# The last two head groups of a gated cross-attention block, run by halves of the batch, with four expert tiles between them

## The chip, the cores and the metric

One core of a Trainium2 chip runs the whole kernel. The metric is the device time of one execution in microseconds (us). The engines are TensorE (PE, matrix products), VectorE (DVE), ScalarE (ACT), GpSimd (POOL) and SyncE (SP), which issues the DMAs. Each executes its own list of instructions in order, and they meet at semaphores.

## The reference

Eight batches of 128 tokens with 512 features. Everything is fp32.

```
x = x + tanh(g_xattn) * attention(layernorm(x), ctx, ctx, pos, mask)
x = x + tanh(g_ffn)  * moe(layernorm(x))

attention: q = h @ Wq (32 heads of 128); k, v = ctx @ Wk, ctx @ Wv (8 heads); rotary on q and k
           softmax(q k' / sqrt(128), masked) v, then @ Wo
moe:       gate = softmax([h, mean|text| / mean|vision|] @ gate_w + gate_b), the two best of 3 experts
           expert e: act_e(h @ w1[e] + b1[e]) @ w2[e] + b2[e],  act = tanh, gelu, silu
           the experts of a batch are those that its token 0 picks
```

## The kernel before

**Products.** Each fp32 operand is kept as a high and a low part (`hi` by ACT, `lo` = value - hi by DVE or POOL), and a product is three products of parts. A tile of 128x512 with an inner size of 512 is twelve matmuls.

**Attention.** The work is cut into 64 *units*: for each of 8 head groups g (one k/v head and its four q heads) the 8 batches. Pass i of the loop `unit(g, par, b, past, drain)` with i = 8g + b handles unit i and older ones, in a pipeline: the q tile of unit i (one head of the group for four batches), the scores of unit i-5 (`LAG_S`), the transposition pt and the product o of unit i-6 (`LAG_P`), and the product y with Wo of unit i-7 (`LAG_Y`), which DVE adds to `xacc`. In a pass PE does, in this order, s(i-5), pt(i-6), q(i), y(i-7), o(i-6). ACT: the high part of o(i-7), a weight chunk, the high parts of q(i-1) and pt(i-6), four exp for s(i-5). DVE: rotation of q(i-1), low part of o(i-7), the scores (add, add, max), low part of pt(i-6), the reciprocal of the exp sums of i-5, `xacc` for i-7. POOL: the sum of the rotation, a weight chunk's low part, the low part of q(i-1), the normalisation of the probabilities of i-5. SP loads a weight chunk and one k/v pair. Group 0 is written out, groups 1 to 6 are a hardware loop over pairs, group 7 and the *drain* (passes 64 to 70, without q) are written out.

**Weights** come in chunks of 128x512 with running numbers n, through four buffers `wraw` (chunk n waits for the low part of chunk n-4). Chunks 20 to 83 are eight for each group: its four Wo chunks, then the next group's four Wq chunks; 80 to 83 are the first expert matrix. From 84 on `EXPERT_ORDER` gives w1[1], w2[0], w1[2], w2[2], w2[1] and w1[0] again. `W_A` = 20, `W_C` = 80. `wa[0..1]` and `wb[0..1]` hold Wq and Wo of two groups.

**The h work** of a batch begins when its last unit is added to `xacc` (unit 56 + b): on DVE statistics (`h_stats`) and mean (`h_neg_mean`), on POOL the power (`h_pow`), on ACT the normalised row (`norm_row`), on PE four transposes (`h_transpose`, here a *turn*), on ACT and DVE its two parts (`h_hi_`, `h_lo_`), and on ACT the sum of |h| (`sum_abs`). Batches 0 to 3 are turned in the banks of q, 4 to 7 in those of s. Before, batch b is turned in pass 65 + b.

**Experts.** `first_layer(l)` is expert *tile* l of 24: tiles 0 to 11 for batches 0 to 3 (four each of tanh, gelu, silu), 12 to 23 for batches 4 to 7 (silu, gelu, tanh). Its activation is `first_act(l)` on ACT. Tile l uses bank l % 2 and waits for activation l-2. `gate_products` and `router` make the gate logits, DVE the scores, `token0` spreads those of token 0 over the partitions, and DVE makes from them the masks that pick experts. `keep` and `pick` on DVE are selects by these masks, `keep_hi_`, `pick_hi_` (ACT), `keep_lo_` (DVE) and `pick_lo_` (POOL) their parts, and the second layer multiplies these by w2. Before, tiles 0 and 1 stand in passes 69 and 70, tiles 2 and 3 between the last turns, and the router behind tile 4.

## Time and profile before

| | |
|---|---|
| median of 3 runs | 737.9 us (737.53 to 738.05) |
| profiled execution | 737.81 us, of which its span 736.0 |
| PE busy | 704.6 us (96%) |
| DVE busy | 558.4 us (76%) |
| POOL busy | 402.6 us (55%) |
| ACT busy | 357.0 us (49%) |
| granted TensorE clock | 0.993 of full speed in the mean |

The span runs from the first to the last instruction of the profiled execution; the time has a little around it. Busy times add up what an engine's instructions took. "PEld" is the weight load of PE, which runs beside its products. Matmuls overlap in the records: the start of one to the start of the next is what it costs.

### The profile page before, as it was taken

How to read it: one execution, taken by the hardware profiler on the slowest of the kernel's cores; microseconds unless marked ns; L12 is line 12 of the kernel's file. 1: busy time of each engine (PE TensorE's matmuls, PEld its weight loads, DVE VectorE, ACT ScalarE, POOL GpSimd, SP SyncE). 2: the span in 40 equal slices, each digit the busy share in tenths (PEclk: the TensorE clock that was granted, in tenths of full speed). 3: DMA queues.
4: the chain of work that ended last, by engine and by line, in shares of the span. 5: the costliest groups of instructions: out<-in, count | busy, mean ns of one | idle time of the engine just before them, and what ended most of it. 6: DMA issues, size and time to landing. Idle time of an engine off the chain costs nothing.

```text
span 736.0 us, 11337 instructions
## 1 busy us (share of the span) xinstructions
PE 704.6 (96%) x3478; PEld 587.7 (80%) x3478; DVE 558.4 (76%) x924; ACT 357.0 (49%) x955; POOL 402.6 (55%) x340
## 2 busy tenths in 40 slices
PE   5798899899999999999999999999999879999998
PEld 3686688688888888888888888888888766788886
DVE  4977778778878787878888887878787984378832
ACT  5522452455554545454545545454545574872130
POOL 5653524665766666666657566666666541383020
PEclk9999999999999999999999999999999999999999
DMA  8695465432133131212213112222222310240101
GB/s 285 223 288 204 171 216 185 129 101 64 52 87 87 58 87 57 82 61 72 71 36 109 58 56 86 86 57 87 58 77 67 104 69 29 58 115 14 58 1 58
DMA packets 66111, 71.10 MB, mean 97 GB/s; under 512 B 8592, under 2 KB 42384, under 8 KB 66064
## 3 DMA queue, kind: packets, MB, share of 16 engines
q1 hardware_dynamic: 65680, 69.51, 30.1%
q0 software_dynamic: 384, 1.05, 0.4%
q8 instruction: 19, 0.31, 0.2%
q14 instruction: 28, 0.23, 0.1%
HBM read 51.66 MB, written 18.87 MB: 96 GB/s over the span
## 4 chain that ended last, share of the span: by engine, by line
PE 82%; DVE 6%; issue 5%; ACT 3%; POOL 3%; DMA 1%; SPq 0%; POOLq 0%; ACTq 0%; DVEq 0%
PE q L263 34%; PE y L253 28%; PE o L590 5%; PE s L542 5%; PE pt L464 4%; PE s L544 2%; PE o L253 1%; PE pt L253 1%; ACT prob L840 1%; POOL roped L1033 1%; DVE rot L1141 1%; DVE rot L1142 1%; DVE rot L1140 1%; DMA wraw<-in_L_xattn_Wk 1%; POOL scores L1033 1%
## 5 line engine op out<-in xcount | busy, mean ns | idle before, releaser
L263 PE MATMUL q<-xT_hi,big 128*128 128x512 f32 x704 | 235.9, 400 | 0.4 <-issue 0.4
L253 PE MATMUL y<-big,split 128*128 128x512 f32 (+1 forms) x784 | 193.0, 392 | 2.9 <-DVE split L1113 2.9
L253 PEld LDWEIGHTS y<-big,split 128*128 128x128 f32 x784 | 147.9, 189 | 34.5 <-DVE split L1113 3.9
L263 PEld LDWEIGHTS q<-xT_hi,big 128*128 128x128 f32 x704 | 132.2, 188 | 27.3 <-issue 0.6
L263 PE MATMUL q<-xT_lo,big 128*128 128x512 f32 x352 | 136.9, 389 | 0.0
L1060 POOL TENSOR_TENSOR roped<-rot 128x512 f32<-128x512 f32 x59 | 76.4, 1295 | 104.1 <-DVE rot L1142 104.1
L840 ACT ACTIVATE prob<-scores,nmax 128x128 f32<-128x128 f32 x256 | 99.8, 391 | 22.2 <-DVE nmax L1245 22.2
L828 ACT ACTIVATE big<-roped 128x512 fp32r<-128x512 f32 x64 | 40.5, 633 | 142.3 <-POOL roped L1060 137.6
L1076 POOL TENSOR_TENSOR prob<-prob,prec 128x512 f32<-128x512 f32 x64 | 66.6, 1040 | 50.7 <-DVE prec L1259 50.7
L1064 POOL TENSOR_TENSOR big<-roped,big 128x512 fp32r<-128x512 f32 x64 | 82.8, 1294 | 13.4 <-ACT big L828 13.4
L1052 POOL TENSOR_TENSOR big<-wraw,big 128x512 fp32r<-128x512 f32 x64 | 83.2, 1300 | 1.9 <-ACT big L820 1.9
L263 PEld LDWEIGHTS q<-xT_lo,big 128*128 128x128 f32 x352 | 66.4, 189 | 12.3
L253 PE MATMUL y<-big 128*128 128x512 f32 (+1 forms) x240 | 60.8, 405 | 8.5 <-DVE split L1113 7.6
L1020 POOL TENSOR_TENSOR big<-wraw,big 128x512 fp32r<-128x512 f32 x36 | 49.3, 1379 | 33.1 <-ACT big L708 33.1
L808 ACT ACTIVATE split<-o 128x512 fp32r<-128x512 f32 x64 | 38.2, 597 | 57.0 <-PE o L590 57.0
L542 PE MATMUL s<-kv,big 128*128 128x256 f32 x256 | 62.6, 322 | 0.0
L1259 DVE RECIPROCAL prec<-psums 128x4 f32<-128x4 f32 x64 | 11.4, 178 | 66.8 <-ACT prob L840 66.5
L253 PEld LDWEIGHTS y<-big 128*128 128x128 f32 x240 | 46.2, 195 | 19.7 <-DVE split L1113 5.1
L1140 DVE TENSOR_TENSOR rot<-q,rope 128x512 f32<-128x512 f32 x80 | 54.6, 682 | 6.2 <-PE q L263 3.1
L263 PE MATMUL q<-big 128*128 128x512 f32 x192 | 50.8, 415 | 8.8 <-DVE big L1113 7.8
L544 PE MATMUL s<-kv,big 128*128 128x128 f32 x256 | 57.0, 223 | 0.0
L1141 DVE TENSOR_TENSOR rot<-q,rope 64x512 f32<-64x512 f32 x80 | 55.4, 693 | 1.1
(170 smaller groups left out, 1141.9 us busy)
## 6 DMA issues: line engine op xcount, KB each, us to landing
k_scratch<-split SPq DMA_DIRECT2D x16, 512.0 KB, 3.5
v_scratch<-split SPq DMA_DIRECT2D x16, 512.0 KB, 3.6
wraw<-in_L_xattn_Wq SPq DMA_DIRECT2D x32, 256.0 KB
wraw<-in_L_xattn_Wo SPq DMA_DIRECT2D x32, 256.0 KB
kv<-k_scratch SPq DMA_DIRECT2D x64, 128.0 KB, 2.5
kv<-v_scratch SPq DMA_DIRECT2D x64, 128.0 KB, 2.8
wraw<-in_L_ffn_w SPq DMA_DIRECT2D x28, 256.0 KB
rows<-ctx_t SPq DMA_DIRECT2D x8, 256.0 KB
```

The lines of the kernel that those rows point to most:

```text
L253: mm = pe.matmul(bank_[:, :], stationary(s, c), moving(m, c), start=(c == 0 and n == 0), stop=(c == EC - 1 and n == 2))
L263: mm = pe.matmul(bank_[:, :].rearrange("p (b t) -> p b t", b=BH), weights[s][:, c, h * P:(h + 1) * P], source[m][:, half * BH:(half + 1) * ...
L542: pe.matmul(sbanks[:, 2 * h * P:(2 * h + 2) * P], q[0], kv[:, bs % NKV, 0:2, :].rearrange("p m k -> p (m k)"), start=True, stop=False)
L544: mm = pe.matmul(sbanks[:, 2 * h * P:(2 * h + 1) * P], q[1], kv[:, bs % NKV, 0, :], start=False, stop=True)
L840: a = act.activation(prob[:, 0, h * P:(h + 1) * P], scores[:, h * P:(h + 1) * P], ACT.Exp, bias=nmax[:, turn, h:h + 1], accum_out=psums[:, ...
L1020: pool.tensor_tensor(buf[1][:, c, :], wraw[:, n % NW, :], buf[0][:, c, :].bitcast(F32), ALU.subtract).then_inc(w_lo, 1)
L1052: pool.tensor_tensor(buf[1][:, b % EC, :], wraw[:, b % NW, :], buf[0][:, b % EC, :].bitcast(F32), ALU.subtract).then_inc(w_lo, 1)
L1060: pool.tensor_tensor(roped[:, :], rot[:, 0, :], rot[:, 1, :], ALU.add).then_inc(q_roped, 1)
L1064: pool.tensor_tensor(q_split(1, bq // BH, bq % HG), roped[:, :], q_split(0, bq // BH, bq % HG).bitcast(F32), ALU.subtract).then_inc(q_lo, 1)
L1076: pool.tensor_tensor(heads(prob[:, 1, :]), heads(prob[:, 0, :]), prec[:, turn, :].unsqueeze(2).to_broadcast([P, HG, P]), ALU.mult).then_in ...
L1140: dve.tensor_tensor(rot[:, 0, :], bank_[:, :], table(0, 0, D), ALU.mult)
L1141: dve.tensor_tensor(rot[0:HALF, 1, :], bank_[HALF:D, :], table(1, HALF, D), ALU.mult)
```

## The change

The last two groups, 6 and 7, are run by halves: units 48 to 51 are group 6 with batches 0 to 3, 52 to 55 group 7 with batches 0 to 3, then 56 to 59 and 60 to 63 the same for batches 4 to 7 (`place`). So batches 0 to 3 have their last unit at 52 to 55 (`last_unit`), four to seven units earlier than before. The weight chunks of these passes come in the order Wq of 7, Wo of 6, Wo of 7 (`TAIL_CHUNKS`, `tail_chunk`). The h work gets tables of its own (`H_STAT` to `H_ABS`): batches 0 to 3 have their statistics in passes 60 to 63, rows in 61 to 64 and turns in 64 and 65. Tiles 0 to 3 go into passes 67 to 70 (`FIRST_AT`), between pt and y. Behind the drain the order on PE and ACT is new, with the router behind tile 7 instead of tile 4. Group 5 and 6 are now written out too.

The diff, cut to what matters; left out are places that only call the new helpers with the batch or buffer of a unit.

```diff
+TAIL = UNITS - 2 * B
+TAIL_CHUNKS = dict(zip(range(TAIL, UNITS), (
+    (68,), (69,), (70, 71), (72,), (73,), (74,), (75,), (76,), (77,), (78,), (79,), (), (80,), (81,), (82,), (83,))))
+H_STAT = {60: 0, 61: 1, 62: 2, 63: 3, 68: 4, 69: 5, 70: 6}
+H_ROW = {61: 0, 62: 1, 63: 2, 64: 3, 69: 4, 70: 5}
+H_TURN = {64: (0, 1), 65: (2, 3), 69: (4,), 70: (5,)}
+H_SPLIT = {65: (0, 1), 66: (2, 3), 70: (4,)}
+H_ABS = {64: (0,), 65: (1, 2), 66: (3,), 70: (4,)}
+FIRST_AT = {67: 0, 68: 1, 69: 2, 70: 3}
...
-        kept = [limit[:, 0:BH, :].rearrange("p b k -> p (b k)"), limit[:, BH:B, :].rearrange("p b k -> p (b k)"),
-                prob[:, 0, :], prob[:, 1, :]]
+        kept = [limit[:, 0:BH, :].rearrange("p b k -> p (b k)"), roped[:, :],
+                limit[:, BH:B, :].rearrange("p b k -> p (b k)"), prob[:, 0, :]]
...
-            with eng.Fori(1, KVH - 2, 2) as g:
+            with eng.Fori(1, KVH - 3, 2) as g:
                 for par in (1, 0):
                     for b in range(B):
                         unit(g + (1 - par), par, b, B, False)
-            for b in range(B):
-                unit(KVH - 1, 1, b, B, False)
+            for n in range(KVH - 3, KVH):
+                for b in range(B):
+                    unit(n, n % 2, b, B, False)
             for b in range(LAG_Y):
                 unit(KVH, 0, b, B, True)
+
+        def place(i):
+
+            if i < TAIL:
+                return i // B, i % B
+            t = (i - TAIL) // BH
+            return KVH - 2 + t % 2, t // 2 * BH + i % BH
+
+        def back(g, par, b, lag):
+
+            if isinstance(g, int):
+                n, batch = place(g * B + b - lag)
+                return n % 2, batch
+            return lagged(par, b, lag)
+
+        def last_unit(hb):
+            return TAIL + BH + hb + (hb >= BH) * BH
...
+        def tail_chunk(n):
+
+            k, c = divmod(n - W_A - TAIL, EC)
+            if k == 0:
+                return Wq[c * P:(c + 1) * P, (KVH - 1) * 512:KVH * 512]
+            if k < 3:
+                row = (KVH - 3 + k) * 512 + c * P
+                return Wo[row:row + P, :]
+            return expert_chunk(n)
+
+        def tail_target(n):
+            k, c = divmod(n - W_A - TAIL, EC)
+            return ((wa[1], c), (wb[0], c), (wb[1], c))[k] if k < 3 else expert_target(n)
...
-                if not drain and past >= EC:
+                if isinstance(g, int) and TAIL <= i < UNITS:
+                    for n in TAIL_CHUNKS[i]:
+                        w_load(n, tail_chunk(n)).then_inc(w_in[n % NW], 16)
+                elif not drain and past >= EC:
                     n = g * W_PER + (W_A + b)
...
-                    if b == 0:
+                    if b == 0 and not (isinstance(g, int) and g == KVH - 1):
                         pe.wait_ge(w_lo, g * W_PER + (W_B + EC))
+                    if isinstance(g, int) and i == TAIL + BH:
+                        pe.wait_ge(w_lo, W_A + TAIL + EC)
                     if past == 0:
...
-                    project_tile(pe, qbank[b % 2], wa[par], b % HG, xT, b // BH).then_inc(q_proj, 1)
+                    pq, bq = back(g, par, b, 0)
+                    project_tile(pe, qbank[b % 2], wa[pq], b % HG, xT, bq // BH).then_inc(q_proj, 1)
...
-                    first_layer(1)
+                if isinstance(g, int) and i in FIRST_AT:
+                    first_layer(FIRST_AT[i])
...
+                    if isinstance(g, int) and i >= TAIL + LAG_Y:
+                        if i - LAG_Y in (TAIL, TAIL + BH):
+                            pe.wait_ge(w_lo, W_A + i - LAG_Y + 2 * EC)
+                    elif b3 == 0:
                         pe.wait_ge(w_lo, g * W_PER + (W_B + W_PER))
...
-                if drain and b >= 1:
-                    h_transpose(b - 1)
-                if drain and b == LAG_Y - 2:
-                    first_layer(0)
+                if isinstance(g, int):
+                    for hb in H_TURN.get(i, ()):
+                        h_transpose(hb)
...
+            first_layer(EC)
             h_transpose(B - 2)
-            first_layer(2)
+            first_layer(EC + 1)
             h_transpose(B - 1)
-            first_layer(3)
+            first_layer(EC + 2)
             gate_products(1)
-            for l in range(EC, NX * EC):
-                first_layer(l)
-                if l == EC:
-                    router()
-                if l == EC + 2:
-                    token0()
+            first_layer(EC + 3)
+            router()
+            first_layer(2 * EC)
+            first_layer(2 * EC + 1)
+            token0()
+            first_layer(2 * EC + 2)
+            first_layer(2 * EC + 3)
...
+                if isinstance(g, int) and TAIL <= i < UNITS:
+                    for n in TAIL_CHUNKS[i]:
+                        w_tail_hi(n)
...
-                    if b >= 1:
-                        norm_row(1, b - 1)
-                    if b >= 2:
-                        h_hi_(b - 2)
-                        sum_abs(b - 2)
-                    if b == LAG_Y - 1:
-                        norm_row(1, b)
-                        h_hi_(b - 1)
-                    if b >= LAG_S:
-                        first_act(b - LAG_S)
+                if isinstance(g, int):
+                    if i in H_ROW:
+                        norm_row(1, H_ROW[i])
+                    for hb in H_SPLIT.get(i, ()):
+                        h_hi_(hb)
+                    for hb in H_ABS.get(i, ()):
+                        sum_abs(hb)
+                    if i in FIRST_AT:
+                        first_act(FIRST_AT[i])
+                if drain and b == LAG_Y - 1:
+                    norm_row(1, B - 2)
+                    h_hi_(B - 3)
...
+            def w_tail_hi(n):
+                if n == W_A + TAIL:
+                    act.wait_ge(q_proj, TAIL)
+                if n == W_A + TAIL + EC:
+                    act.wait_ge(y_done, TAIL - B)
+                if n == W_A + TAIL + 2 * EC:
+                    act.wait_ge(y_done, TAIL)
+                if n >= W_C:
+                    w_expert_hi(n)
+                else:
+                    buf, k = tail_target(n)
+                    w_split_hi(n, n % NW, buf[0][:, k, :])
+
             def w_expert_hi(n):
+                if n == W_C:
+                    act.wait_ge(q_proj, UNITS - BH)
                 if n == W_C + EC:
                     act.wait_ge(q_proj, UNITS)
                 if n == W_C + 2 * EC:
-                    act.wait_ge(y_done, UNITS - B)
+                    act.wait_ge(y_done, UNITS - BH)
                 if n == W_C + 3 * EC:
...
                 if l == 0:
+                    act.wait_ge(s_part, UNITS - B)
+                if l == 1:
+                    act.wait_ge(q_lo, UNITS)
+                if l == 2:
                     act.wait_ge(s_part, UNITS)
-                if l == 2:
+                if l == 3:
                     act.wait_ge(p_t, UNITS)
-                if l == EC:
-                    act.wait_ge(h_t, B)
-                    act.wait_ge(h_abs, B)
+                if EC <= l < 2 * EC:
+                    act.wait_ge(h_t, B - EC + f + 1)
+                    act.wait_ge(h_abs, B - EC + f + 1)
...
             h_hi_(B - 2)
             norm_row(1, B - 1)
+            gate_copy(0)
+            sum_abs(B - 3)
+            first_act(EC)
             w_expert_hi(n)
-            gate_copy(0)
-            first_act(2)
+            sum_abs(B - 2)
             h_hi_(B - 1)
-            for b in range(B - 3, B):
-                sum_abs(b)
-            first_act(3)
+            first_act(EC + 1)
+            sum_abs(B - 1)
             w_expert_hi(n + 1)
+            first_act(EC + 2)
+            w_expert_hi(n + 2)
             gate_copy(1)
-            w_expert_hi(n + 2)
-            first_act(4)
+            w_expert_hi(n + 3)
+            first_act(EC + 3)
+            w_expert_hi(n + 4)
             act.wait_ge(score_exp_in, 1)
             act.activation(exps, logit, ACT.Exp).then_inc(score_exp, 1)
-            w_expert_hi(n + 3)
-            first_act(5)
-            w_expert_hi(n + 4)
             w_expert_hi(n + 5)
-            first_act(6)
             w_expert_hi(n + 6)
-            first_act(7)
+            first_act(8)
             w_expert_hi(n + 7)
-            w_expert_hi(n + 8)
-            first_act(8)
             keep_hi_(0)
             keep_hi_(1)
+            w_expert_hi(n + 8)
+            first_act(9)
             w_expert_hi(n + 9)
-            first_act(9)
             pick_hi_(0)
...
+                        if isinstance(g, int) and TAIL <= i < UNITS:
+                            for n in TAIL_CHUNKS[i]:
+                                w_split_lo(n, *tail_target(n))
...
+                    if i in H_STAT:
+                        h_pow(H_STAT[i])
...
+                if isinstance(g, int):
+                    if i in H_ROW:
+                        h_neg_mean(H_ROW[i])
+                    if i in H_STAT:
+                        h_stats(H_STAT[i])
+                if drain and b == LAG_Y - 1:
+                    h_neg_mean(B - 2)
...
-                if drain and b >= 2:
-                    h_lo_(b - 2)
+                if isinstance(g, int):
+                    for hb in H_SPLIT.get(i, ()):
+                        h_lo_(hb)
```

## Rows read from the trace of the kernel before

**Rows 1.** The page, part 1: busy us, share of the span, instructions.

```profile
PE 704.6 (96%) x3478; PEld 587.7 (80%) x3478; DVE 558.4 (76%) x924; ACT 357.0 (49%) x955; POOL 402.6 (55%) x340
```

**Rows 2.** Windows: us, busy time of each engine, granted clock, DMA share, GB/s.

```profile
100.00:571.00 471.00, 467.99 (x2419) 398.32 (x2418) 384.96 (x621) 239.49 (x726) 297.87 (x246) 1.00 0.27 82
571.00:627.00 56.00, 48.19 (x243) 37.66 (x242) 40.20 (x83) 34.41 (x91) 21.85 (x24) 0.97 0.21 67
627.00:667.00 40.00, 40.00 (x189) 32.46 (x188) 23.92 (x62) 27.59 (x47) 22.25 (x17) 1.00 0.31 86
```

**Rows 3.** Timeline of pass 63: start, us, instruction, [idle before <- releaser]; DVE, ACT, POOL.

```profile
562.86 0.18 DVE L1259 RECIPROCAL prec<-psums 128x4 f32<-128x4 f32 x1 [1.12 <-ACT prob L840]
...
563.79 0.60 ACT L808 ACTIVATE split<-o 128x512 fp32r<-128x512 f32 x1 [0.95 <-PE o L590]
...
555.63 1.04 POOL L1076 TENSOR_TENSOR prob<-prob,prec 128x512 f32<-128x512 f32 x1 [0.87 <-DVE prec L1259]
...
563.12 1.04 POOL L1076 TENSOR_TENSOR prob<-prob,prec 128x512 f32<-128x512 f32 x1 [0.87 <-DVE prec L1259]
```

**Rows 4.** Timeline of PE in the drain and just behind it.

```profile
574.12 3.00 PE L253 MATMUL y<-big,split 128*128 128x512 f32 x12 [1.57 <-DVE split L1113]
...
589.88 0.66 PE L464 MATMUL q<-ident,rows 128*128 128x128 f32 x4 [0.72 <-ACT rows L724]
...
605.65 4.60 PE L253 MATMUL y<-big,split 128*128 128x512 f32 x12 [0.72 <-DVE split L1113]
...
623.57 0.63 PE L464 MATMUL s<-ident,rows 128*128 128x128 f32 x4 [1.09 <-DVE xT_lo L1113]
```

**Rows 5.** Windows of PE alone: us, busy (x), granted clock, DMA share, GB/s.

```profile
77.26:80.20 2.94, 0.00 (x0) 1.00 0.27 110
80.20:83.65 3.45, 3.03 (x7) 0.51 0.40 152
572.60:574.10 1.50, 0.00 (x0) 1.00 0.70 193
...
605.90:609.30 3.40, 3.40 (x9) 0.50 0.23 84
```

**Rows 6.** Timeline of DVE and ACT in the drain.

```profile
576.63 0.68 DVE L1275 BATCH_NORM_STATS2 bn<-xacc 128x6 f32<-128x512 f32 x1
...
595.89 0.18 DVE L1259 RECIPROCAL prec<-psums 128x4 f32<-128x4 f32 x1
...
589.03 0.80 ACT L724 ACTIVATE rows<-xacc,nmr,rstd 128x512 f32<-128x512 f32 x1
589.74 0.57 ACT L890 ACTIVATE xT_hi<-q 128x512 fp32r<-128x512 f32 x1
590.22 0.62 ACT L885 ACTIVATE rope<-rows 128x512 f32<-128x512 f32 x1
...
594.21 0.40 ACT L840 ACTIVATE prob<-scores,nmax 128x128 f32<-128x128 f32 x1 [1.71 <-DVE nmax L1245]
```

**Rows 7.** Timeline of PE: first s of pass 64, first products of the second layer.

```profile
571.07 0.28 PE L542 MATMUL s<-kv,big 128*128 128x256 f32 x1
...
667.25 4.92 PE L253 MATMUL y<-big 128*128 x21
```

**Rows 8.** Timeline of DVE, ACT and POOL from the router to the picked tiles.

```profile
637.16 0.17 DVE L1309 TENSOR_SCALAR scores<-s 128x8 f32<-128x8 f32 x1 [8.30 <-PE s L673]
...
642.93 0.18 DVE L1355 COPY scores<-s 128x24 f32<-128x24 f32 x1 [1.27 <-PE s L679]
...
646.53 1.37 DVE L1382 COPY_PREDICATED limit<-s,rows 128x512 f32<-128x512 int32 x2
...
639.71 1.28 ACT L914 ACT_TABLE_LOAD   x1
641.01 0.69 ACT L914 ACTIVATE rows<-q,b1c 128x512 f32<-128x512 f32 x1
...
649.32 1.14 ACT L924 ACTIVATE big<-limit 128x512 fp32r<-128x512 f32 x2
...
659.25 1.29 POOL L1093 TENSOR_TENSOR split<-rot,kv 128x512 fp32r<-128x512 f32 x1
```

More of the change, by code:

```diff
@@ L321, in build @@
         gate_rows = [rot[0:8, hf, :] for hf in range(2)]
-        def is_last(g, b):
-            return isinstance(g, int) and g == KVH - 1
         def bcast(row, n):
@@ L432, in unit @@
                 if past >= LAG_S + KV_FIRST and (not drain or b < LAG_S):
-                    _, bj = lagged(par, b, LAG_S)
-                    gj = g if b >= LAG_S else g - 1
+                    slot = lagged(par, b, LAG_S)[1] % NKV
+                    if isinstance(g, int):
+                        gj, bj = place(i - LAG_S)
+                    else:
+                        gj, bj = g if b >= LAG_S else g - 1, (b - LAG_S) % B
                     if past - LAG_S >= NKV or past == B:
@@ L438, in unit @@
                             sp.wait_ge(o_done, i - LAG_S - NKV + 1 + (b == 0))
-                    load_kv(sp, bj % NKV, gj, bj)
+                    load_kv(sp, slot, gj, bj)
                 if past in VALUES_AT:
@@ L808, in unit @@
                     act.activation(split[:, 2, 0, :], obank[:, :], ACT.Copy).then_inc(o_hi, 1)
-                if not drain:
+                if isinstance(g, int) and TAIL <= i < UNITS:
+                    for n in TAIL_CHUNKS[i]:
+                        w_tail_hi(n)
+                elif not drain:
                     if b == 0 and past >= B:
@@ L842, in unit @@
                     a.then_inc(s_exp, 1)
-                if drain:
-                    if b >= 1:
-                        norm_row(1, b - 1)
-                    if b >= 2:
-                        h_hi_(b - 2)
-                        sum_abs(b - 2)
-                    if b == LAG_Y - 1:
-                        norm_row(1, b)
-                        h_hi_(b - 1)
-                    if b >= LAG_S:
-                        first_act(b - LAG_S)
+                if isinstance(g, int):
[10 more added lines that the diff above has]
+                    h_hi_(B - 3)
             def s_done_before(t, bq):
                 return t - bq % BH - BH + (bq == B - 1)
+            def w_tail_hi(n):
[7 more added lines that the diff above has]
+                    w_expert_hi(n)
+                else:
+                    buf, k = tail_target(n)
+                    w_split_hi(n, n % NW, buf[0][:, k, :])
             def w_expert_hi(n):
+                if n == W_C:
+                    act.wait_ge(q_proj, UNITS - BH)
                 if n == W_C + EC:
@@ L1060, in unit @@
                         pool.tensor_tensor(roped[:, :], rot[:, 0, :], rot[:, 1, :], ALU.add).then_inc(q_roped, 1)
-                        if not drain:
+                        if isinstance(g, int) and TAIL <= i < UNITS:
+                            for n in TAIL_CHUNKS[i]:
+                                w_split_lo(n, *tail_target(n))
+                        elif not drain:
                             weight_lo()
@@ L1069, in unit @@
                     w_expert_lo(W_A + KVH * W_PER + b)
-                    h_pow(b)
+                    if i in H_STAT:
+                        h_pow(H_STAT[i])
                 if has(LAG_S):
@@ L1078, in unit @@
                                        ).then_inc(p_norm, 1)
-                if drain:
-                    if b == LAG_Y - 1:
-                        h_pow(B - 1)
+                if not drain and isinstance(g, int) and i in H_STAT:
+                    h_pow(H_STAT[i])
+                if drain and b == LAG_Y - 1:
+                    h_pow(B - 1)
             def h_pow(hb):
@@ L1220, in unit @@
                         dve.wait_ge(q_roped, i - 1)
-                    rotate(qbank[bq % 2], bq // BH, q_rot)
+                    rotate(qbank[bq % 2], back(g, par, b, 1)[1] // BH, q_rot)
                     if past == 1:
@@ L1235, in unit @@
                 if has(LAG_S):
-                    turn, bs = (b - LAG_S) % 2, (b - LAG_S) % B
+                    turn, bs = (b - LAG_S) % 2, back(g, par, b, LAG_S)[1]
                     dve.wait_ge(s_done, i - LAG_S + 1)
@@ L1249, in unit @@
                     subtract_hi(split[:, 1, 1, :], pbank[:, :], split[:, 1, 0, :], p_lo)
-                if drain:
-                    if b >= 1:
-                        h_neg_mean(b - 1)
-                    h_stats(b)
-                    if b == LAG_Y - 1:
-                        h_neg_mean(b)
+                if isinstance(g, int):
[3 more added lines that the diff above has]
+                        h_stats(H_STAT[i])
+                if drain and b == LAG_Y - 1:
+                    h_neg_mean(B - 2)
                 if has(LAG_S):
@@ L1260, in unit @@
                 if has(LAG_Y):
-                    b3 = (b - LAG_Y) % B
+                    turn, b3 = (b - LAG_Y) % 2, back(g, par, b, LAG_Y)[1]
                     dve.wait_ge(y_done, i - LAG_Y + 1)
-                    dve.scalar_tensor_tensor(out=xacc[:, b3, :], in0=ybank[b3 % 2][:, :], scalar=gates[:, 0:1],
+                    dve.scalar_tensor_tensor(out=xacc[:, b3, :], in0=ybank[turn][:, :], scalar=gates[:, 0:1],
                                              in1=xacc[:, b3, :], op0=ALU.mult, op1=ALU.add).then_inc(y_acc, 1)
-                if drain and b >= 2:
-                    h_lo_(b - 2)
+                if isinstance(g, int):
+                    for hb in H_SPLIT.get(i, ()):
+                        h_lo_(hb)
             def h_lo_(hb):
@@ L1272, in h_stats @@
             def h_stats(hb):
-                dve.wait_ge(y_acc, UNITS - B + hb + 1)
+                dve.wait_ge(y_acc, last_unit(hb) + 1)
                 dve.bn_stats(bn[:, 1, hb, :], xacc[:, hb, :]).then_inc(h_step, 1)
```

6 lines of the change are left out of this document (2 added, 4 removed).

## The prediction

> **What bounds the kernel now.** I read the page first: TensorE (PE) is busy for 704.6 of 736.0 us [rows 1]. The windows by stage say where the rest is [rows 2]: from 100 to 571 us PE is idle for 3.0 us, from 627 to 667 never, and between 571 and 627, the drain (passes 64 to 70, with no q projection left), it is busy for 48.2 of 56 us, partly at a low clock. I then followed the drain in order of time, engine by engine [rows 4, 6], and the router stage behind it [rows 8]. In a steady pass PE has no gap, VectorE (DVE), ScalarE (ACT) and GpSimd (POOL) have gaps of 1.12, 0.95 and 0.87 us beside others, and a pass takes 7.49 us (POOL's normalisations start so far apart) [rows 3]. So two things can matter: the gaps of the drain, and new ones behind it.
>
> I compare by one ledger, from the start of s in pass 64 (571.07) to that of the second layer (667.25), 96.18 us [rows 7]. PE's work in it is the same in both kernels: 5 s of 0.93, 6 pt of 0.40, 7 y and 16 expert tiles of 2.72 to 2.84, 6 o of 0.68, 8 turns (h transposes) of 0.40, 2 gate products of 1.84, the router's 2.41, token0's 0.14; together 84.2. Lost: 12.0. The largest pieces are 1.57 before y(57), several of 0.7 before turns, 1.09, and 1.9 for the twelve products of y(62), which took 4.60 instead of 2.72 [rows 4] since the granted clock was 0.50, the 1.2 GHz level, from 605.9 to 609.3 [rows 5].
>
> **Up to pass 63: +0.14.** The new order of units keeps counts, sizes and lags, so a PE pass stays at 7.49. Wq chunks are ready two passes ahead (71 in POOL's pass 50, wanted in 52), Wo chunks one (75 in 54, wanted by y in 55), as the last Wq chunk was before: 0. SP has the kv pair and one weight DMA a pass, two in pass 50 and none in 59, and runs about three passes ahead: 0. In pass 50 POOL splits two chunks, 1.26 more against the 0.87 idle before its normalisation; this then ends 0.14 after the moment at which PE wants it. In passes 60 to 63 DVE gets statistics (0.72+0.22+0.15) and a mean (0.07), 1.15 in its gap of 1.12, which ends with the same exp (pass 64 of before carries the statistics in that place and the reciprocal is on time); ACT gets a row of 0.71 in 0.95: 0 [rows 3, 6]. Without these gaps each would cost its length four times.
>
> **The drain.** I laid out the new list of each engine with these durations: on ACT o split 0.49, weight split 0.52, p split 0.58, exp set 1.56 (1.68 until DVE's reciprocal), row 0.71, h split 0.48, |h| sum 0.61; on DVE 0.60 to 0.72 an operation; POOL's normalisation 1.04, started 0.25 after the reciprocal [rows 3, 6]. On the clock of before:
> - Pass 64: y(57) waits 1.57 as before. Two turns follow instead of none.
> - Pass 65: ACT does row 3 and |h| 0 ahead of the split of o(58), which starts at 579.02: y(58) at 580.39, gap 0.66. Turns 2 and 3 need h_lo 0 and 1, which DVE has only behind its reciprocal and xacc(58), at 585.53 and 586.13: gaps 1.64 and 0.21.
> - Pass 67: pt(61) waits 0.61 for POOL, tile 0 waits 0.38 for h_lo 3 (593.62).
> - Passes 67 to 70 each have a tile of 2.84 between pt and y, which covers the chain o, ACT, DVE, y of 1.4, and the scores behind it: no gap. Tile 3 ends at 618.96, y(63) at 621.68.
>
> Sum 5.07: here the change wins 7 us.
>
> **Behind the drain.** Tile 4 is a Gelu. ACT does h split 6, row 7, gate copy, |h| 5, a table load (1.28 [rows 8]) and then the Gelu: from the end of turn 6 (625.58) that lasts until 629.96. PE is through tile 5 and turn 7 at 628.5 and needs the bank for tile 6: 1.5 lost. The router ends at 639.73. Tile 8, now right behind it, needs weight chunk 95, which ACT splits behind the Gelu of tile 7 and POOL finishes at 640.14: 0.45 lost.
>
> **The large one, tile 11.** PE's order is router, 8, 9, token0, 10, 11. Tile 11 overwrites the bank of tile 9 and needs its activation. On ACT this stands behind keep_hi(0) and keep_hi(1), these wait for DVE's selects, the selects for the masks, the masks for token0. Before, from the router's result at 637.16 to the copy of token0's took 5.77, from that copy to the first select 3.60, and keep_hi came at 649.32, held up by nothing [rows 8]. Now the router's result lands at 639.77; token0 stands behind tile 9, so the copy is at 646.05, the first select from 649.65 to 650.40, keep_hi at 650.42 and 651.05, the split of chunk 99, then the activation from 652.09 to 652.78. PE has only tiles 8, 9 and 10 (8.3) for the 13.1 between router and tile 11. It is through at 648.60 and goes on at 652.83: 4.23 lost. What is late next: POOL ends chunk 99 at 653.5, chunk 100 at 654.74 and the first pick_lo (1.29) at 656.03 [rows 8]; the activation of tile 10 waits for that and ends at 656.75, so tile 12 starts at 656.8 instead of 655.6: 1.2 lost. From tile 13 on the activations are early.
>
> The clock: 3 us of idle at 77.3 were followed by a stretch at 0.50, 1.5 us at 572.6 weren't [rows 5]. The hole of 4.2 will bring such a stretch. 3.4 us of it lose 1.7, of which 1.2 fall into the wait of tile 12: 0.5, with bounds of 0 (hidden) and 1.2 (a longer stretch).
>
> **Sum.** 5.07+1.5+0.45+4.23+1.2 = 12.45 lost against 12.0: +0.5; clock +0.5; pass 50 +0.14: +1.1. The second layer begins at 668.4 instead of 667.25; behind it PE is the bound in both, and DVE had 2.69 to spare before the first product. The profiled execution took 737.81 (span 736.0 and 1.81 around it); +1.1 is 738.9. The median of the runs, 737.9, lies 0.09 above the profiled one. That is slower by 0.15%, inside the 0.2% (1.5 us) that a measurement of this kernel can tell from no change.
>
> The Trainium skill, "ScalarE: Activation LUTs", section "What ACT_TABLE_LOAD costs", gives a switch of the table set a drain of about 1.38 us beside the load of 1283 ns. The trace agrees with the load, not with the drain: behind the load at 639.71 the next activation starts at 641.01 [rows 8]. By the page tile 6 would wait 1.4 longer; the sum goes by the rows.
>
> **Rivals.**
> 1. *Tile 11 doesn't wait*: its activation gets ahead of the selects, or these come sooner. For it: before, this chain never stopped PE. Against: the order on ACT, and the 9.4 from router to select. Without 4.23, 1.2 and 0.5 it gives 733.0, faster. It would need the first select by 646. Chance 0.13.
> 2. *The clock falls in the drain too*, behind the gaps at 584 to 586 or at 592 to 594, as at 605.9 of before, behind gaps each under 0.8 [rows 4, 5]. It lengthens a y or a tile by up to 1.9, the end by 1.1 to 1.9: 740.0 to 740.8, slower. It is decided by whether one of these gaps is followed by 0.50. Chance 0.15.
> 3. *A table load has a drain where ACT's queue is full*, as the page has it: tile 6 waits 2.9, 740.3. Chance 0.05.
> 4. *The added work of DVE doesn't fit*: in passes 60 to 66 each pass is 0.2 to 0.3 longer, as gap and work are nearly equal: 740.3 to 741. Chance 0.10.
> 5. The ledger holds: 738.9, its own range 737.4 to 740.4. Chance 0.57: 0.03 below, 0.40 within, 0.14 above the 0.2%.
>
> Faster 0.16 (rival 1 and the 0.03), same 0.45 (0.40 and 0.05 of rivals 2 and 4 where other waits cover them), slower 0.39 (the rest). The range leaves out most of rival 1 and the far end of 2 and 4: 735.5 to 741.2.
>
> **What the profile after should show.** PE without a gap up to pass 63 but for 0.14; gaps of 1.6 before y(57) and before turn 2, none in passes 68 to 70; y(63) done near 622 as before, but with four tiles done instead of two; a wait of 1.5 at tile 6 behind a table load; ACT idle for 5 us before the first keep_hi, PE for 4 us before tile 11, then a clock of 0.50. I am wrong if the second layer starts before 666, or if tile 11 waits less than 3.

## The result, and the profile after

The changed kernel took 739.1 us in the median of 13 runs (737.93 to 740.43), the kernel before 737.09 in as many beside them (735.09 to 740.49): a ratio of 1.0029, interval 1.0017 to 1.0041. So it is 0.3% slower, about 2 us; the lower end of the interval lies just under the 0.2% that a measurement can tell from no change, the middle above it. The profiled executions are 1.12 apart, 738.93 (span 737.2) against 737.81.

The page, part 1, and the windows of the changed kernel, with the columns of [rows 1] and [rows 2]:

```profile
PE 707.2 (96%) x3478; PEld 590.4 (80%) x3478; DVE 558.0 (76%) x924; ACT 355.4 (48%) x954; POOL 403.7 (55%) x340
```
```profile
100.00:571.00 471.00, 468.98 (x2418) 399.48 (x2416) 388.76 (x635) 241.78 (x730) 298.79 (x249) 1.00 0.28 82
571.00:627.00 56.00, 51.94 (x270) 42.27 (x269) 36.26 (x68) 32.63 (x88) 20.16 (x20) 1.00 0.23 67
627.00:667.00 40.00, 36.22 (x154) 27.59 (x153) 22.05 (x60) 25.58 (x45) 22.90 (x17) 0.91 0.28 86
```

Subtract the busy time of PE from the length of each window. In the drain PE was idle for 7.8 us [rows 2] and is now idle for 4.1; behind it, it was never idle and is now idle for 3.8. The idle time of the two stretches is 7.8 in both kernels: all of it that the drain gave up came back 50 us later. What is left is the clock, 0.97 in one stretch before, 0.91 in the other now: one piece at half speed against two. By the ledger of the prediction, pass 64 now starts at 570.78 and the second layer at 668.45, 97.67 against 96.18: 1.49 longer, and one piece of half clock, 3.4 us long, costs about 1.6 (y(62) took 4.60 in [rows 4], the other y after a wait 3.00). So without the clock the two kernels are level here.

Timeline of PE, changed kernel: every wait over 0.15 from the drain to the second layer's start, and that start.

```profile
573.99 3.02 PE L262 MATMUL y<-big,split 128*128 128x512 f32 x12 [1.58 <-DVE split L1191]
...
580.25 3.02 PE L262 MATMUL y<-big,split 128*128 128x512 f32 x12 [0.34 <-DVE split L1191]
...
585.51 1.22 PE L506 MATMUL q<-ident,rows 128*128 128x128 f32 x8 [1.55 <-DVE xT_lo L1191]
...
592.86 0.66 PE L506 MATMUL pt<-ident,prob 128*128 128x128 f32 x4 [0.49 <-POOL prob L1153]
...
629.98 0.50 PE L272 MATMUL q<-xT_hi,big 128*128 128x512 f32 x1 [1.27 <-ACT rows L988]
...
640.22 0.79 PE L272 MATMUL q<-xT_hi,big 128*128 128x512 f32 x1 [0.22 <-POOL big L1093]
...
652.25 0.50 PE L272 MATMUL q<-xT_hi,big 128*128 128x512 f32 x1 [1.79 <-ACT rot L988]
...
656.84 0.59 PE L272 MATMUL q<-xT_hi,big 128*128 128x512 f32 x1 [0.29 <-ACT rot L988]
...
660.15 0.50 PE L272 MATMUL q<-xT_hi,big 128*128 128x512 f32 x1 [0.20 <-ACT rot L988]
...
668.45 3.79 PE L262 MATMUL y<-big 128*128 x16
```

The first four lines are y(57), y(58), turn 2 and pt(61), against the list of [rows 4]: between pt(61) and tile 6 there is no wait over 0.15. The next five are tiles 6, 8, 11, 12 and 13. Windows of PE alone give the two pieces of low clock, columns as in [rows 5]:

```profile
640.00:643.40 3.40, 3.18 (x9) 0.51 0.23 77
653.80:657.20 3.40, 3.11 (x8) 0.51 0.46 154
```

The second follows the hole before tile 11. The first lies on tile 8 and begins right behind the router, whose sixteen small products (8 by 4) had run since 637.52; the sum had no term for it.

The chain that holds tile 11, in the timelines of DVE and ACT (the places of [rows 8]):

```profile
640.04 0.17 DVE L1389 TENSOR_SCALAR scores<-s 128x8 f32<-128x8 f32 x1 [7.78 <-PE s L722]
...
647.74 0.18 DVE L1435 COPY scores<-s 128x24 f32<-128x24 f32 x1 [2.23 <-PE s L728]
647.95 0.54 DVE L1385 TENSOR_TENSOR scores<-scores 128x16 f32<-128x16 f32 x4
...
649.09 0.74 DVE L1462 COPY_PREDICATED limit<-s,rows 128x512 f32<-128x512 int32 x1
```
```profile
627.94 1.28 ACT L988 ACT_TABLE_LOAD   x1
629.24 0.69 ACT L988 ACTIVATE rows<-q,b1c 128x512 f32<-128x512 f32 x1
...
649.92 0.63 ACT L998 ACTIVATE big<-limit 128x512 fp32r<-128x512 f32 x1 [3.93 <-DVE limit L1462]
650.48 0.63 ACT L998 ACTIVATE big<-roped 128x512 fp32r<-128x512 f32 x1
651.01 0.61 ACT L759 ACTIVATE big<-wraw 128x512 fp32r<-128x512 f32 x1
651.53 0.67 ACT L988 ACTIVATE rot<-q,b1c 128x512 f32<-128x512 f32 x1
```

ACT stands for 3.93 at the first `keep_hi`, and the activation of tile 9, which PE wants, is third in the row behind it. It ends at 652.20 and tile 11 starts at 652.25.

### The profile page after: what moved, and what is told of

The parts are those of the page before. It is cut to its first block, busy times and chain, and to the rows that moved or that the text cites. A ratio compares the mean times of both kernels' runs of the same rounds, so it can differ in the third digit from the quotient of the medians.

```text
span 737.2 us, 11089 instructions
## 1 busy us (share of the span) xinstructions
PE 707.2 (96%) x3478; PEld 590.4 (80%) x3478; DVE 558.0 (76%) x924; ACT 355.4 (48%) x954; POOL 403.7 (55%) x340
## 4 chain that ended last, share of the span: by engine, by line
PE 79%; DVE 8%; issue 4%; POOL 4%; ACT 2%; DMA 1%; SPq 0%; ACTq 0%; POOLq 0%; DVEq 0%
PE q L272 32%; PE y L262 28%; PE o L640 5%; PE s L584 5%; PE pt L506 4%; PE s L586 2%; PE o L262 1%; PE pt L262 1%; POOL big L1093 1%; DVE rot L1219 1%; DVE rot L1220 1%; DVE rot L1218 1%; POOL roped L1106 1%; DMA wraw<-in_L_xattn_Wk 1%; DVE split L1191 1%
## 5 line engine op out<-in xcount | busy, mean ns | idle before, releaser
L272 PE MATMUL q<-xT_hi,big 128*128 128x512 f32 x704 | 240.8, 406 | 3.9 <-ACT rot L988 2.3
L272 PEld LDWEIGHTS q<-xT_hi,big 128*128 128x128 f32 x704 | 134.2, 191 | 33.4 <-ACT rot L988 2.8
L272 PE MATMUL q<-xT_lo,big 128*128 128x512 f32 x352 | 138.6, 394 | 0.0
L1342 DVE SCALAR_TENSOR_TENSOR xacc<-y,gates,xacc 128x512 f32<-128x512 f32 x64 | 47.9, 748 | 13.3 <-PE y L262 9.5
```

The source lines that it names most:

```text
L272: mm = pe.matmul(bank_[:, :].rearrange("p (b t) -> p b t", b=BH), weights[s][:, c, h * P:(h + 1) * P], source[m][:, half * BH:(half + 1) * ...
L1342: dve.scalar_tensor_tensor(out=xacc[:, b3, :], in0=ybank[turn][:, :], scalar=gates[:, 0:1], in1=xacc[:, b3, :], op0=ALU.mult, op1=ALU.add) ...
```

## The experiments

All times are medians, compared with the kernel before on the same chip; ratios have their 95% interval. What a single profiled execution says of a wait is read by the prediction's ledger, from the first s of pass 64 to the second layer, with the number of half-clock pieces in it; a table of all of them stands behind experiment 9. The whole time of one such execution also holds the pieces ahead of pass 64, one to four of them, so it is not used alone.

**1. The activation of tile 9 ahead of the selects' parts.**

```diff
             w_expert_hi(n + 7)
+            first_act(9)
             keep_hi_(0)
             keep_hi_(1)
             w_expert_hi(n + 8)
-            first_act(9)
```

> The changed kernel with one edit: ScalarE does the activation of tile 9 ahead of keep_hi 0 and 1, so that tile 11 does not wait for the router's masks. My theory (the drain's gain is given back behind it, mostly at tile 11): the 1.8 us wait before tile 11 goes, and with it the 1.2 GHz stretch behind it that lengthened tile 11 by 1.4 and the small waits of tiles 12 and 13; some 3 to 4 us less than the changed kernel, 735.5. Rival (the unit order of passes 48 to 63 or the written-out code costs the time): no change, 739. Rival 2 (the chain behind tile 9 moves the wait on to tile 12, whose activation needs POOL's first pick_lo): only 1 us less.

Measured: 740.2 in 5 runs (739.6 to 740.85), 1.0052 (1.0038 to 1.0066), so not faster than the changed kernel; the 3 to 4 us of the theory did not come, and neither did the 1 us of rival 2, though its mechanism did. Tile 11 no longer waits; tile 12 does. PE, ACT and POOL of this run:

```profile
656.82 0.77 PE L272 MATMUL q<-xT_hi,big 128*128 128x512 f32 x1 [4.04 <-ACT rot L988]
```
```profile
655.99 0.69 ACT L988 ACTIVATE rot<-q,b1c 128x512 f32<-128x512 f32 x1 [0.62 <-POOL split L1171]
```
```profile
651.69 2.98 POOL L1093 TENSOR_TENSOR big<-wraw,big 128x512 fp32r<-128x512 f32 x2 [3.62 <-ACT big L759]
654.63 1.26 POOL L1171 TENSOR_TENSOR split<-rot,kv 128x512 fp32r<-128x512 f32 x1
```

Follow it backwards: tile 12 waits for the activation of tile 10, this for `pick_lo`(0) on POOL (its buffer), which stands behind the low parts of two weight chunks, which wait for ACT, which waits for the selects. The theory that the order on ACT costs these microseconds fell: the wait is a property of the whole chain from the router to the activation of tile 10, and removing its first place moves it to the second.

**2. The Gelu of tile 4 first.**

```diff
             n = W_A + KVH * W_PER + LAG_Y
+            first_act(EC)
             h_hi_(B - 2)
             norm_row(1, B - 1)
             gate_copy(0)
             sum_abs(B - 3)
-            first_act(EC)
```

> The changed kernel with one edit: the first Gelu activation (tile 4) stands ahead of h split 6, so its table load falls into the 2.6 us in which ScalarE waits for turn 6. Theory: the 1.3 us wait before tile 6 goes; all behind it comes 1.3 earlier: 737.8. Rival (a table load is followed by a drain of its own, or the wait before tile 6 is only replaced by one before turn 7, whose row is now 0.6 later): no gain.

Measured: 737.78 in 11 runs, 1.0016 (1.0006 to 1.0026). The wait of tile 6 is gone. The median is 1.3 lower than that of the changed kernel, 0.8 lower when each is set against the kernel before in its own session (+1.2 for +2.0). In the profiled execution PE is idle for 2.8 us behind the drain instead of 3.8, so 1.0 of the 1.27 comes through. Tile 11 then waits 2.16. (That the profiled executions are 1.15 apart says little: this one has one piece of half clock less behind the drain and came to pass 64 1.5 us later.)

```profile
627.00:667.00 40.00, 37.21 (x166) 28.67 (x165) 24.23 (x62) 25.35 (x46) 22.94 (x17) 0.96 0.30 86
```

**3. The order of units alone.** Units, weight chunks and written-out groups as changed; h work, tiles and all behind the drain as before. The core of its difference to the changed kernel:

```diff
-FIRST_AT = {67: 0, 68: 1, 69: 2, 70: 3}
...
+H_TURN = {UNITS + b: (b - 1,) for b in range(1, LAG_Y)}
...
+H_ABS = H_SPLIT
+FIRST_AT = {69: 0, 70: 1}
...
+            for l in range(EC, NX * EC):
+                first_layer(l)
+                if l == EC:
+                    router()
+                if l == EC + 2:
+                    token0()
```

> Only the unit order of the last two groups, the weight order and the written-out group 5 and 6 of the change; the h work, the tiles and the router stay where they were before. Theory: worth nothing, within 0.3 us of before (PE in passes 48 to 63 has no gap but 0.1). Rival (the order of units or the written-out code costs): 1 to 2 us above before, and the whole of the difference between the two kernels is here.

Measured: 736.7 in 11 runs, 1.0006 (0.9996 to 1.0017). The new order of units costs or gives nothing by itself that could be told from noise (the interval leaves room for 1.3 us), and its ledger is 96.15 for the 96.18 of before; what changes the time is where h work and tiles stand.

**4. Four waits mended at once.** Experiments 1 and 2 together, the split of chunk 95 ahead of the activation of tile 7, and `token0` behind tile 8:

```diff
             first_layer(2 * EC)
-            first_layer(2 * EC + 1)
             token0()
+            first_layer(2 * EC + 1)
...
-            first_act(EC + 3)
             w_expert_hi(n + 4)
+            first_act(EC + 3)
```

> The changed kernel with four edits of order: both of the above, weight chunk 95 split ahead of the activation of tile 7, and token0 right behind tile 8. Theory: the waits before tiles 6 (1.3), 8 (0.2), 11 (1.8), 12 and 13 (0.5) and the 1.2 GHz stretch behind tile 11 (1.4) go: 5 us below the changed kernel, 734, clearly below before. Rival: the gain of the drain itself is small, and this comes out no better than before, 737.

Measured: 738.03 in 11 runs, 1.0025 (1.0013 to 1.0036); the theory had 734. PE of this run, and the two ends of the chain on DVE and ACT:

```profile
653.94 0.47 PE L272 MATMUL q<-xT_hi,big 128*128 128x512 f32 x1 [2.91 <-ACT rot L988]
...
657.24 0.50 PE L272 MATMUL q<-xT_hi,big 128*128 128x512 f32 x1 [0.30 <-ACT rot L988]
```
```profile
638.22 0.17 DVE L1389 TENSOR_SCALAR scores<-s 128x8 f32<-128x8 f32 x1 [8.10 <-PE s L722]
...
653.11 0.69 ACT L988 ACTIVATE rot<-q,b1c 128x512 f32<-128x512 f32 x1 [0.63 <-POOL split L1171]
```

With these short cuts in place, the router's result is on DVE at 638.22 and the activation of tile 10 is done at 653.80: 15.6 us. Between the router and tile 12 PE has tiles 8 to 11, 10.9 us. The 4.7 that are missing are mostly the wait of 2.91 and a piece of half clock on tile 8 (638.4 to 641.9, about 1.6), which filled some of the hole with slow work. Before, seven tiles stood there (5 to 11). By the ledger four mended waits gave no more than the one of experiment 2: 95.07 and 95.00, one piece of half clock in each.

**5. A shorter chain, with more work under it.** On top of 2: the router one tile earlier and `token0` behind tile 7, on ACT and POOL the selects' parts ahead of weight chunks that are not urgent, and five small DVE operations on the gate weights behind the last pick (in experiment 4 they took 2.74 us in the middle of the chain). The order of the selects and their low parts on DVE changed a little too. These are many edits in one run: what each of them gives was not separated.

```diff
-            first_layer(EC + 3)
             router()
+            first_layer(EC + 3)
+            token0()
             first_layer(2 * EC)
             first_layer(2 * EC + 1)
-            token0()
...
             keep_hi_(0)
             keep_hi_(1)
-            w_expert_hi(n + 8)
-            first_act(9)
-            w_expert_hi(n + 9)
             pick_hi_(0)
+            first_act(9)
+            w_expert_hi(n + 6)
+            w_expert_hi(n + 7)
...
-            for j in range(9):
+            for j in range(6):
                 w_expert_lo(n + j)
+            pick_lo_(0)
...
```

> The changed kernel with the chain from router to tile 12 shortened from both ends: the router ahead of tile 7, token0 behind tile 7, VectorE's five small operations that the masks do not need moved behind the last pick, the first picked tile split by ScalarE and GpSimd ahead of weight chunks 97 to 100, the Gelu of tile 4 first. Theory as it stands after the first four (tiles 0 to 3 in the drain were the cover of the chain router, masks, select, pick_hi, pick_lo, activation 10, tile 12, which takes 15.5 us against 10.9 us of tiles 8 to 11): chain about 12, cover 13.6, so no wait before tile 11 or 12, only 0.6 before the router for its gate copy; 733.5 to 735, 4 to 5 us under the changed kernel. Rival (what is lost is not this chain but half-clock stretches that come anyway, whichever wait is there): 737.5 or more.

Measured: 734.62 in 12 runs (731.34 to 736.31), 0.9969 (0.995 to 0.9988): faster than before, though the upper end of the interval is only 0.1% off. Against the kernel before of its own session it is 2.0 lower, where the changed kernel was 2.0 higher: 4.0 between them. From 627 to 667 PE has two waits left, 0.72 before the router and 0.23 before one tile (658.05). The drain's own gaps are those of the changed kernel (1.58, 0.32, 1.53, 0.48), and one piece of half clock is left (637.3 to 640.8).

```profile
634.38 1.91 PE L718 MATMUL s<-fold,rot 8*128 8x4 f32 x16 [0.72 <-issue]
...
658.05 0.50 PE L272 MATMUL q<-xT_hi,big 128*128 128x512 f32 x1 [0.23 <-ACT limit L988]
```
```profile
571.00:627.00 56.00, 51.99 (x270) 42.29 (x269) 36.27 (x68) 34.13 (x90) 20.53 (x20) 1.00 0.23 67
627.00:667.00 40.00, 39.05 (x177) 31.10 (x176) 26.58 (x63) 28.68 (x51) 24.57 (x19) 0.96 0.30 86
```

**6 and 8. Does POOL slow the small operations of DVE?** In the changed kernel the first select came 1.35 after the copy, before 3.60 [rows 8]. POOL ran beside it before (642.29 to 646.1) and stood idle after (647.4 to 651.7). One chunk (6, n + 8 alone), then two (8, as shown), were put ahead of `keep_hi_(0)`, so that POOL is busy there again:

```diff
             w_expert_hi(n + 7)
+            w_expert_hi(n + 8)
+            w_expert_hi(n + 9)
             keep_hi_(0)
             keep_hi_(1)
-            w_expert_hi(n + 8)
             first_act(9)
-            w_expert_hi(n + 9)
```

> The changed kernel with chunk 99 split ahead of keep_hi 0 instead of behind keep_hi 1, so that GpSimd works while VectorE makes the masks. It measures why the copy of token0's result to the first select took 3.60 us before and 1.35 after, with the same eleven small operations. Theory: small VectorE operations wait for a GpSimd tensor_tensor that is under way (1.3 each); the 1.35 becomes 2.3 or more. Rival (the difference lies in the clock or in semaphores): 1.35 stays.

> The changed kernel with chunks 99 and 100 both split ahead of keep_hi 0, so that GpSimd works from 646.2 to about 651, all through VectorE's mask operations (with chunk 99 alone it was done 0.5 us after they began). Theory: while a GpSimd tensor_tensor runs, small VectorE operations wait; copy to first select, 1.35 in the changed kernel and 1.51 with chunk 99 alone, becomes 2.5 to 3.6. Rival: stays at 1.4.

One profiled execution each. In 6 POOL was already done at 648.71, half a microsecond after the copy, and the first select came after 1.51: inconclusive, as the overlap was missing. In 8 POOL ran on. DVE and POOL of 8:

```profile
647.52 0.18 DVE L1435 COPY scores<-s 128x24 f32<-128x24 f32 x1 [2.05 <-PE s L728]
647.74 2.05 DVE L1385 TENSOR_TENSOR scores<-scores 128x16 f32<-128x16 f32 x4
...
650.38 0.73 DVE L1462 COPY_PREDICATED limit<-s,rows 128x512 f32<-128x512 int32 x1
```
```profile
645.88 3.79 POOL L1093 TENSOR_TENSOR big<-wraw,big 128x512 fp32r<-128x512 f32 x3 [0.72 <-ACT big L759]
```

The same four operations take 2.05 instead of 0.54, and copy to select takes 2.86. The edit moves work of ACT as well, but ACT stands idle from 647.14 to 651.20 here and from 645.99 to 649.92 in the changed kernel, so POOL is what differs beside these operations. Tile 11 then waits 2.77; the end does not move by it (ledger 97.66, the changed kernel 97.67), since POOL then has those two chunks behind it and begins the first `pick_lo` at 653.55 instead of 654.64.

**7. The early h work with the cover left in place.** Tiles 0 and 1 in passes 69 and 70 and the order behind the drain as before; the turns of batches 0 to 3 early.

```diff
-FIRST_AT = {67: 0, 68: 1, 69: 2, 70: 3}
+FIRST_AT = {69: 0, 70: 1}
...
             h_transpose(B - 2)
-            first_layer(EC + 1)
+            first_layer(2)
             h_transpose(B - 1)
-            first_layer(EC + 2)
+            first_layer(3)
```

> The unit order and the early h work of batches 0 to 3 as changed, but only tiles 0 and 1 in the drain (passes 69 and 70) and the router behind tile 4, with both tails as before. Theory: the drain loses some 2 us more than in the changed kernel (no cover in passes 67 and 68) but 4 less than before, and the router's chain keeps its cover of seven tiles, so no wait behind it: 3 to 4 us under before, 733 to 734. Rival (the drain's gain comes only with the tiles in it, the early h work is worth nothing): as before, 736.6.

Measured: 735.74 in 12 runs (734.65 to 738.17), 0.9984 (0.9966 to 1.0003), not told apart from before. PE has no idle time from 627 to 667, so with three more tiles between the router and tile 12 (5 to 11 instead of 8 to 11) the chain is covered. In the drain it is idle for 7.3, 0.5 less than before, and the profiled run has two pieces at half clock instead of one: y(57) took 4.62 for 3.0, and the other lies behind the router (635.7 to 639.2).

```profile
573.39 4.62 PE L262 MATMUL y<-big,split 128*128 128x512 f32 x12 [1.58 <-DVE split L1190]
```
```profile
571.00:627.00 56.00, 48.70 (x246) 39.03 (x246) 36.04 (x68) 34.40 (x91) 20.73 (x21) 0.97 0.25 67
627.00:667.00 40.00, 40.00 (x180) 32.25 (x179) 22.91 (x61) 25.55 (x43) 21.26 (x16) 0.96 0.30 85
```

The expected saving of 3 to 4 did not come: passes 67 to 69 have gaps again (0.79, 0.45, 1.32) and turn 6 waits 1.10. By the ledger, 96.41 with two pieces against 96.18 with one, the early h work saves some 1.4, and the second piece hides it.

**9. Turns 2 and 3 one pass later.** On top of 5:

```diff
-H_TURN = {64: (0, 1), 65: (2, 3), 69: (4,), 70: (5,)}
+H_TURN = {64: (0, 1), 66: (2, 3), 69: (4,), 70: (5,)}
-H_ABS = {64: (0,), 65: (1, 2), 66: (3,), 70: (4,)}
+H_ABS = {66: (0,), 67: (1,), 68: (2,), 69: (3,), 70: (4,)}
```

> The kernel of e5_router_early with the turns of batches 2 and 3 at the end of pass 66 instead of 65 and the |h| sums spread over passes 66 to 70. Theory: the wait of 1.55 before turn 2 goes and the split of o(58) and o(59) come 0.6 and 1.2 earlier; some waits of pass 66 take part of it: 1 us under e5, 733.5. Rival (the passes without a tile are bound by the chain scores, exp, reciprocal, normalisation, pt in any case): as e5, 734.6.

Measured: 732.32 in 10 runs (730.97 to 736.28), 0.9952 (0.9932 to 0.9973). This is the lowest median, 4.6 under the kernel before. It is 2.3 under that of experiment 5, but the two intervals overlap, and the ten runs lie in two groups, six from 731.0 to 732.5 (mean clock 0.990 to 0.995) and four from 735.6 to 736.3 (0.986 to 0.988). PE and the windows of the profiled execution, which is one of the first group:

```profile
574.37 3.03 PE L262 MATMUL y<-big,split 128*128 128x512 f32 x12 [1.59 <-DVE split L1199]
...
585.07 0.66 PE L506 MATMUL pt<-ident,prob 128*128 128x128 f32 x4 [0.47 <-POOL prob L1153]
...
586.38 3.02 PE L262 MATMUL y<-big,split 128*128 128x512 f32 x12 [0.66 <-DVE split L1199]
...
633.02 1.91 PE L718 MATMUL s<-fold,rot 8*128 8x4 f32 x16 [0.72 <-issue]
```
```profile
571.00:627.00 56.00, 52.99 (x276) 43.55 (x275) 36.57 (x68) 35.59 (x94) 20.50 (x20) 1.00 0.24 67
627.00:667.00 40.00, 39.02 (x183) 31.02 (x181) 28.04 (x65) 28.10 (x48) 27.23 (x20) 1.00 0.29 86
```

Idle 3.0 and 1.0, against 7.8 and 0 before and 4.1 and 3.8 after the change; the profiled run has no piece at half clock in these two windows. The wait of 1.55 before turn 2 is gone, and the change keeps the drain's gain almost without paying behind it. Against experiment 5 the ledger is 2.74 shorter, of which 1.6 is the piece of half clock that this execution does not have; 1.1 is what the edit gave, about the 1 us expected.

**All profiled executions by the ledger.** The last column takes off 1.6 us for each piece of half clock, an estimate from y(57), which took 4.61 and 4.62 with such a piece on it and 3.0 without.

| kernel | pass 64 at | second layer at | ledger | pieces in it | without them |
|---|---|---|---|---|---|
| before | 571.07 | 667.25 | 96.18 | 1 | 94.6 |
| changed | 570.78 | 668.45 | 97.67 | 2 | 94.5 |
| 1 | 570.91 | 669.39 | 98.48 | 2 | 95.3 |
| 2 | 572.29 | 667.29 | 95.00 | 1 | 93.4 |
| 3 | 570.71 | 666.86 | 96.15 | 1 | 94.6 |
| 4 | 570.51 | 665.58 | 95.07 | 1 | 93.5 |
| 5 | 571.10 | 663.62 | 92.52 | 1 | 90.9 |
| 6 | 570.14 | 668.44 | 98.30 | 2 | 95.1 |
| 7 | 570.16 | 666.57 | 96.41 | 2 | 93.2 |
| 8 | 570.71 | 668.37 | 97.66 | 2 | 94.5 |
| 9 | 571.15 | 660.93 | 89.78 | 0 | 89.8 |

## Why the prediction was right in sum, and where its steps were not

*Up to pass 63.* Around pass 50 pt starts 7.59 apart instead of 7.49: 0.10 for 0.14. Pass 64 starts at 570.78, 0.29 earlier than before where 0.14 later was forecast; the nine kernels of the experiments start it between 570.1 and 571.2, one of them at 572.29, so this is within their spread. No other edit shows a cost, and experiment 3 says the same of the whole order of units.

*The drain.* The prediction counts a wait from the moment at which the product before it would have let the next one start; the profile's idle time begins only when that product has ended, some 0.2 us later (pt is 0.66 long and costs 0.40). So the profile's 4.1 of idle time must not be set against 5.07. From start to start the gaps are 1.84, 0.56, 1.72 (+0.18) and 0.59 (+0.36), 5.25 in all, predicted 1.57, 0.66, 1.64 (+0.21) and 0.61 (+0.38), 5.07; no gap in passes 68 to 70. By 621.7 PE has done two tiles more than before, 5.5 us of work; the rest of the 7 us is mostly the wait of 1.09 behind the drain, which is gone. It won what it was to win.

*Tile 6 and tile 8.* From start to start 1.48 for 1.5 and 0.29 for 0.45 (1.27 and 0.22 in the profile); experiment 2 shows that some 1 us of the first reaches the end. Behind the load at 627.94 the activation starts 1.30 later, the load alone, as in [rows 8]. Rival 3 did not occur.

*Tiles 11 to 13.* Here a term was mis-sized. The prediction had 4.23 and 1.2; measured are 1.79 (1.95 from start to start), then 0.29 and 0.20. It also said "I am wrong if ... tile 11 waits less than 3", and tile 11 waits less than 3. The mechanism holds: the activation of tile 9 does stand behind both `keep_hi`, which wait for the selects, and it ends at 652.20 where 652.78 was laid out. Two sizes were off. The step from the copy to the first select was taken over from [rows 8] as 3.60, but it was that long because POOL ran beside it, and in the new order POOL is idle: 1.35 (shown by experiment 8). And PE was ready for tile 11 1.7 later, at 650.30 instead of 648.60, nearly all of it because of a piece of half clock on tile 8, which the sum did not have: tiles 8 and 9 took 7.11 for 5.56. Tile 11, on the second piece, and the wait of tile 12 took 1.75 over the 2.84 of a tile, and tile 12 with the wait of tile 13 0.47. From the router to tile 13 the loss is thus 0.29 + 1.55 + 1.95 + 1.75 + 0.47 = 6.0, where 0.45 + 4.23 + 1.2 + 0.5 = 6.4 was laid out: nearly the same size, but half of it slow work and not waiting. That is luck, and so is the total: the ledger grew by 1.49 for 0.95, and the start of pass 64 moved by -0.29 for +0.14, which together give the second layer +1.20 for +1.1.

*The clock.* It fell once where predicted, behind the hole at tile 11 (653.8), and once behind the router. Rival 2 had it in the drain; the kind of event was right, the place wrong. Experiments 1, 6 and 7 show a form of it in the drain (y(57) took 4.61 to 4.62, behind the same wait of 1.58 that had no such effect in the profiles of the changed kernel and of the other experiments).

*The router's chain as the price of the move.* The forecast priced the two places where it would show. Experiments 1 and 4 show that it is one chain of 15.6 us that needs as much work of PE under it, 7 says that with three more tiles behind the router it is covered, and 5 and 9 say that the gain is there once the chain is shortened and started earlier. The rival of experiment 5, that the loss is half-clock pieces which come whichever wait is there, is not borne out: without its piece, experiment 5 is 3.6 shorter than the changed kernel without its two.

*Rivals 1 and 4.* Tile 11 waits, though less than forecast, so rival 1 (733.0) did not come; its ingredient, an earlier select, came in part, and what it gave was spent on the clock. For rival 4, DVE would have made passes 60 to 66 longer: s of pass 64 starts 0.29 earlier than before, not later, and the gaps of passes 64 to 66 are those laid out.

*The size of the median.* The medians differ by 2.0 where the profiled executions differ by 1.1. The two kernels spread over 2.5 and 5.4 us from run to run, and in experiment 5 the runs go with the mean granted clock: 731.3 at 0.998, 734.0 in the mean at 0.993, 735.3 at 0.988. The profiled execution of the kernel before has three pieces of half clock in its whole span and a mean clock of 0.993, that of the changed kernel five and 0.988. The mean over the runs was 0.990 for the changed kernel and 0.992 for the one before (27 runs, beside experiments 1 to 4). That more low-clock pieces fall behind the new holes would fit; which holes bring them in the runs without a profile was not seen, and it stays open.

## What to carry to other kernels

Before work is moved forward into idle time, ask what that work covered at its old place: measure the longest chain of the other engines that starts and ends on the main engine there (here 15.6 us from router to tile 12), and leave as much work between its ends. If one wait of such a chain is removed and the next one on it grows by as much, stop reordering and shorten the chain or start it earlier. And a duration copied from a trace belongs to its surroundings: if the change removes the neighbour that ran beside it, the duration changes too.

## What the runs showed of the hardware

Small DVE operations (0.16 to 0.2 us alone) take up to 1.2 while POOL runs an elementwise operation of 128x512 (the low part of a weight chunk): four of them 1.81 in the kernel before, 0.54 with POOL idle after the change, 2.05 in experiment 8 with POOL busy again. It hits a cast with a single input too; DVE of experiment 5, while a POOL operation ran from 642.60 to 643.88:

```profile
642.67 1.23 DVE L1447 CAST pick_row<-scores 128x8 int32<-128x8 f32 x1
643.82 0.16 DVE L1448 TENSOR_SCALAR pick_row<-scores 128x8 int32<-128x8 f32 x1
```

It ends when POOL's does. The Trainium skill, "SBUF — State Buffer", section "Who interferes with whom", says that DVE with two SBUF inputs, or with one in a mode that uses both port pairs, shares a pair with GpSimd, and that whoever comes first holds it for the whole instruction. The traces agree: here DVE waits out one operation of 1.28. Whether this cast runs in such a mode they do not show.

Half clock also comes where no hole of PE is near: behind the router's 16 tiny products in the changed kernel (640.0 to 643.4) and in experiment 4 (638.4 to 641.9), with no wait over 0.3 since 630 in the one and since 593 in the other. It came 2.3 to 4.1 us behind their start in six of the eleven profiles (the changed kernel and experiments 4 to 8) and in none of the other five, though all have the same products. That the products are its cause is not shown: no run leaves them out. The wait of 1.56 to 1.59 before y(57) is the same kind of case: it was followed by half clock in three of the eleven.
